# A relational graph layer on one core: products of a tile's end two triples earlier, an edgeless triple left out, a clearing moved, and a small read put ahead of the weights

## The reference

```python
x, src, dst, edge_type = ...      # x [6250, 256]; 200000 edges, sorted by dst; 8 edge types
def gnn(x, edge_index, edge_type, W_rel, W_root, bias):    # three layers
    for l in range(3):
        xr = einsum('nd,rde->rne', x, W_rel[l])
        msg = xr[edge_type, src]
        agg = segment_sum(msg, dst, num_segments=6250)
        x = relu(agg + x @ W_root[l] + bias[l])
    return x
def ffn(x, weight, bias):         # a product through logarithms
    log_x, log_w = log(|x| + 1e-8), log(|weight| + 1e-8)
    acc = exp(log_x - mx) @ exp(log_w - mw).T              # mx, mw: row maxima
    sign = sign(sign(x) @ sign(weight).T)
    return sign * exp(log(acc) + mx + mw.T) + bias
x = x + gnn(layernorm(x), (src, dst), edge_type, ...)
out = x + ffn(layernorm(x), ffn_weight, ffn_bias)
```

## Time and profile before

| | us |
|---|---|
| median of three runs | 6018.02 |
| the three runs | 6017.11 to 6022.20 |
| the profiled execution | 6019.02 |
| its span, first to last instruction | 6017.1 |
| busy: GpSimd | 4448.2 (74%) |
| busy: TensorE, products / weight loads | 4364.5 (73%) / 3933.9 (65%) |
| busy: VectorE | 1827.8 (30%) |
| busy: ScalarE | 619.2 (10%) |
| HBM traffic over the span | 112 GB/s |

### The profile page before, as it was taken

How to read it: one execution, slowest core, us unless ns; L and a number is a source line. 1 busy time by engine, 2 the same in 40 slices (tenths; PEclk the granted TensorE clock), 3 DMA queues, 4 the chain that set the end, 5 groups by cost and what they waited for, 6 DMA issues and landing times.

```text
span 6017.1 us, 84648 instructions
## 1 busy us (share of the span) xinstructions
PE 4364.5 (73%) x26040; PEld 3933.9 (65%) x26041; DVE 1827.8 (30%) x3533; ACT 619.2 (10%) x848; POOL 4448.2 (74%) x4715
## 2 busy tenths in 40 slices
PE   4777777777787777777777767767777777677776
PEld 3666666666676666666666666656666666666666
DVE  4222222222222222222222222223334334333333
ACT  3010010101010000010001000001011011101111
POOL 5777777777777677777777777767777777777775
PEclk9898988898989889898989898988888888888888
DMA  6333333333333333333333333333333333333332
GB/s 194 113 111 113 112 113 111 113 112 113 112 113 112 105 109 108 108 110 107 109 108 109 108 108 109 108 107 110 110 111 112 111 111 113 111 110 113 110 111 84
DMA packets 284200, 672.46 MB, mean 112 GB/s; under 512 B 79916, under 2 KB 133905, under 8 KB 284082
## 3 DMA queue, kind: packets, MB, share of 16 engines
q0 software_dynamic: 225072, 614.90, 35.7%
q1 hardware_dynamic: 30308, 30.00, 1.6%
q10 hardware_dynamic: 28702, 26.46, 1.3%
HBM read 645.36 MB, written 25.68 MB: 112 GB/s over the span
## 4 chain that ended last, share of the span: by engine, by line
POOL 42%; PE 26%; issue 18%; DMA 9%; ACT 2%; DVE 2%; DVEq 2%; ACTq 0%; SPq 0%; POOLq 0%
POOL rows L373 42%; PE bank L391 14%; PE bank L450 10%; DMA rows<-node_table,idx 8%; ACT agg L666 2%; DVE agg L945 1%; PE bank L569 1%; DVE onehot L865 0%; PE bank L495 0%; DVEq L928 0%; DVEq L931 0%; PE bank L567 0%; DVEq L1035 0%; ACT x_in L622 0%; DVEq L945 0%
## 5 line engine op out<-in xcount | busy, mean ns | idle before, releaser
L373 POOL DMA_INDIRECT rows<-node_table,idx x4689 | 4440.9, 947 | 1519.4 <-issue 1316.0
L391 PE MATMUL bank<-onehot,rows 128*128 128x128 f32 x18792 | 2764.7, 308 | 1472.3 <-DMA rows<-node_table,idx 712.8
L391 PEld LDWEIGHTS bank<-onehot,rows 128*128 128x128 f32 x18792 | 2598.6, 220 | 1648.1 <-issue 1629.9
L945 DVE TENSOR_TENSOR agg<-bank,agg 128x256 f32 x1566 | 664.1, 424 | 2172.6 <-PE bank L391 1656.4
L450 PE MATMUL bank<-wrel,agg 128*128 128x256 f32 x5568 | 1273.9, 388 | 14.8 <-issue 8.7
L450 PEld LDWEIGHTS bank<-wrel,agg 128*128 128x128 f32 x5568 | 1079.0, 197 | 164.1 <-issue 17.4
L865 DVE TENSOR_TENSOR onehot<-bank,key 128x1152 f32<-128x1152 f32 x525 | 707.2, 1347 | 0.0
L666 ACT COPY agg<-zero_col 128x2304 f32 x174 | 367.2, 2111 | 3082.4 <-PE bank L450 3082.4
L967 DVE SCALAR_TENSOR_TENSOR acc<-bank,in_first,acc 128x256 f32 x174 | 84.2, 484 | 1897.2 <-PE bank L450 1768.8
L569 PE MATMUL bank<-wroot,nextT 128*128 128x256 f32 x392 | 147.4, 512 | 0.0
L673 ACT COPY acc<-bank 128x256 f32 (+1 forms) x98 | 36.5, 372 | 1052.6 <-PE bank L569 1052.6
(11 more groups left out here) (137 smaller groups left out, 751.6 us busy)
## 6 DMA issues: line engine op xcount, KB each, us to landing
rows<-node_table,idx POOLq DMA_INDIRECT x4689, 2.7
node_table<-new_x ACTq DMA_DIRECT2D x98, 128.0 KB
x_tile<-node_table SPq DMA_DIRECT2D x58, 128.0 KB, 2.2
x_in<-in_x_dram SPq DMA_DIRECT2D x8, 768.0 KB, 11.2
wrel<-in_L_gnn_W_rel_dram SPq DMA_DIRECT2D x6, 1024.0 KB, 7.5
xres<-in_x_dram ACTq DMA_DIRECT2D x48, 128.0 KB
out_dram<-res ACTq DMA_DIRECT2D x48, 128.0 KB
node_table<-x_in SPq DMA_DIRECT2D x7, 768.0 KB, 8.1
```

What stands on the lines that cost most here:

```text
L373: pool.indirect_dma_start(rows[:, s:s + D], None, tables[layer % 2], bass.IndirectOffsetOnAxis(ap=idx[:, g * TPG + k, j:j + 1], axis=0),). ...
L391: last = nc.tensor.matmul(to[:, h, :], of[:, s:s + P], hot[:, hot_k * CH + j, :], start=(j == 0), stop=(j == CH - 1))
L945: nc.vector.tensor_tensor(window, seg[k % 3].rearrange("p h (r w) -> p h r w", r=R), window, ALU.add).then_inc(agg_added, 1)
```

## The change

Five edits, with the bookkeeping of the semaphores for them:

- SyncE reads the triples' span back (58 x 9 values, twice) directly behind its store, ahead of the first layer's weights and the root weights.
- VectorE clears all of agg behind the first one-hots, and not ahead of the feed-forward weights' preparation.
- TensorE has the transposes of a tile's end behind triple 3 (BATCH) and its products behind triple 5 (BATCH + 2), and not behind 4 and 7; layer 0's own two go with them.
- Triple 8 of the last group is not multiplied and not added: TensorE and VectorE only count their semaphores on. In layers 0 and 1 VectorE folds the last group's window ahead of making the next one-hots.
- ScalarE's clearing moves from the end of its part of a group to its start, and clears the half whose transform has just run. It stands so behind new_x and not in front of it.

```diff
@@ SyncE
             sp.dma_start(span_dram.rearrange("m (b p) -> (m b) p", p=P), span_rows[:, :]).then_inc(span_stored, 16)
+            sp.wait_ge(span_stored, 16)
+            for m in range(2):
+                sp.dma_start(span9[:, m, :], span_dram[m, 0:TRIPLES].rearrange("(g k) -> g k", k=TPG)).then_inc(span_loaded, 16)
 
             sp.wait_ge(turned, 11)
             load_weights(0)
...
-            sp.wait_ge(span_stored, 16)
-            for m in range(2):
-                sp.dma_start(span9[:, m, :], span_dram[m, 0:TRIPLES].rearrange("(g k) -> g k", k=TPG)).then_inc(span_loaded, 16)
...
-                sp.wait_ge(out_ready, (layer + 1) * GROUPS)
+                sp.wait_ge(out_ready, (layer + 1) * GROUPS + 1)
@@ TensorE
+            pe.sem_inc(out_ready, 1)
...
+                    if k == TPG - 1:
+
+                        with pe.If(g < GROUPS - 1):
+                            pe.wait_ge(gathered[k], g * (16 * CH) + (layer * (GROUPS - 1) * (16 * CH) + 16 * CH))
+                            pe.wait_ge(agg_added, n + 1)
+                            pe.sem_inc(pe_mark, 1)
+                            products(seg[k % 3], rows, onehot[:, k // BATCH, :, :], k, k % BATCH).then_inc(seg_ready, 1)
+                        with pe.Else():
+                            pe.wait_ge(agg_added, n + 3)
+                            pe.sem_inc(seg_ready, 1)
+                        pe.sem_inc(pe_mark, 1)
+                        continue
...
-                    if late and k == TPG // 2:
+                    if late and k == BATCH:
                         with pe.If(g < late[0]):
                             turn_ended(layer, late[1])
-                    if late and k == TPG - 2:
+                    if late and k == BATCH + 2:
                         with pe.If(g < late[0]):
                             multiply_ended(layer, late[1])
-                    if layer == 0 and k == TPG // 2:
+                    if layer == 0 and k == BATCH:
                         turn(gg)
-                    if layer == 0 and k == TPG - 2:
+                    if layer == 0 and k == BATCH + 2:
@@ ScalarE
                 gg = g + layer * GROUPS
+
+                act.wait_ge(out_ready, gg + 1)
+                act.sem_inc(act_mark, 1)
+                nc.scalar.copy(agg[:, ds((g + 1) % 2 * KH, KH), :, :].rearrange("p h r s -> p (h r s)"),
+                               zero_col[:, :].to_broadcast([P, KH * R * SLOTS])).then_inc(agg_zeroed, 1)
...
-                act.wait_ge(out_ready, gg + 1)
-                act.sem_inc(act_mark, 1)
-                nc.scalar.copy(agg[:, ds(g % 2 * KH, KH), :, :].rearrange("p h r s -> p (h r s)"),
-                               zero_col[:, :].to_broadcast([P, KH * R * SLOTS])).then_inc(agg_zeroed, 1)
@@ VectorE
-            nc.vector.memset(agg[:, :, :, :], 0.0).then_inc(agg_zeroed, 2)
             dve.wait_ge(ffn_loaded, 16)
...
                 make_onehots(0, b).then_inc(onehot_ready, 1)
 
+            nc.vector.memset(agg[:, :, :, :], 0.0).then_inc(agg_zeroed, 1)
...
+                last_group = layer < L - 1 and g == GROUPS - 1
...
+                    def no_edge():
+
+                        dve.wait_ge(agg_added, n + 3)
+                        dve.sem_inc(agg_added, 1)
+
+                    if k < TPG - 1:
+                        add()
+                    elif layer < L - 1:
+                        (add if g < GROUPS - 1 else no_edge)()
+                    else:
+                        with dve.If(g < GROUPS - 1):
+                            add()
+                        with dve.Else():
+                            no_edge()
+                        dve.sem_inc(dve_mark, 1)
+                    if k % BATCH == BATCH - 1 and not (k == TPG - 1 and last_group):
                         make_onehots(g + 1, k // BATCH).then_inc(onehot_ready, 1)
...
                 nc.vector.tensor_tensor(agg[:, half, :, 0:WIN], agg[:, half, :, 0:WIN], agg[:, half, :, P:SLOTS], ALU.add).then_inc(agg_ready, 1)
+                if last_group:
+                    make_onehots(g + 1, BATCHES - 1).then_inc(onehot_ready, 1)
...
-                dve.wait_ge(out_ready, gg + 1)
+                dve.wait_ge(out_ready, gg + 2)
```

## The result

| | before | after |
|---|---|---|
| median, us | 6020.35 (22 runs, 6012.06 to 6024.10) | 6012.24 (22 runs, 6004.08 to 6016.27) |
| ratio | | 0.9985, 95% interval 0.9978 to 0.9991 |
| profiled execution / span, us | 6019.02 / 6017.1 | 6014.94 / 6013.0 |

The change gains 9 us (0.15%, and by the interval between 5 and 13 us). The gain is real, but 22 us were forecast, and the time lies outside the predicted range of 5989 to 6008. Three executions of other rounds took 6312, 7301 and 16894 us; the medians and ratios of this document leave them out.

What follows compares the result with a forecast made beforehand. GpSimd's gather stream (4689 steps of 1.25 us) was taken to bound the kernel, 97% of the span. 6019.0 - 6.8 (head) - 15.9 (ends) + 1.0 (tail) = 5997.3, less 1.0 for the median: 5996 us, range 5989 to 6008.

Steps and rivals of the forecast that it cites:

- The head, 6.8: Before the steady gather stream: earlier span read and later agg clearing shorten GpSimd's 7.49 us ring stall by 6.8, bounds 3 to 7.19.
- The two ends, 15.9: Ends of layers 0 and 1: transforms start 7.2 and 6.7 us earlier, clearing's move gives 2.0; bounds 12 to 17.5.
- ScalarE's clearing: Behind the transform at each layer end: new_x no longer waits for agg's clearing, 1.0 us gained each time.
- the 4.6 us of moved products: End of layer 0: products taken from in front of the transform, 2.3 us hidden in TensorE's idling, 2.3 pushing k=6.
- Inside the layers, gathers: Gathers lengthened by VectorE's all-SBUF instructions: net change 0, bounds 6.9 us less to 16.6 more.
- Rival 3: Last layer's 49 tile ends: shifted operations lengthen gathers; three hits each give 6025 us. Chance 0.03, at half price 0.05.
- Inside the layers, the place of the transposes: Last layer's tile ends: TensorE idles some 2.5 us more waiting for mag, but the ring covers it, cost 0.
- the prediction's signs of being wrong: GpSimd waits over 0.4 us elsewhere, last layer's gathers summing over 1495 us, or table waits over 20 us.
- The tail, +1.0: After the last gather: mag at 5977.0 and the following work equal, 1.0 us added for TensorE's clock; bounds -0.5 to 2.6.
- Rival 4, the ring empties: Last layer: beyond 8.4 us of lag each us costs 48 us; 1 us over gives 6044. Chance 0.02.

Runs made afterwards that it cites:

- the run with the head alone: Kernel before with only the triples' span read ahead of the weights and agg cleared behind the first one-hots: 6020.61 us, ratio 0.9987.

## Why the prediction was wrong

- **The head, 6.8.** Right. 6.4 in one profile, 5.1 in the other; 4.1 (where it was alone) to 7.2 in the others that have the edit. The reload and TensorE's start, on which it hung, came within 0.6 us of their forecast in the first profile and within 1.6 in the second.
- **The two ends, 15.9.** Nearly right: 14.7 and 11.7. The terms for the products and for ScalarE's clearing were right (0.9 of 1.0); missed were 1.0 us of the sequencer's way, and the clock: the sum took 7.14 us for both transforms, but in the twelve profiles layer 0's took it four times and layer 1's eight times, and otherwise 8.1 to 10.0 us. Part of the near hit is luck: the 4.6 us of moved products were read from a profile in which they ran at half clock, and the run with the head alone has ends 4.7 us shorter with nothing changed there. Measured against those, the change's ends gained 10.0 and 7.0 us.
- **Inside the layers, gathers.** The 0 stood: the gathers of the last layer over 0.97 us number 66 before and 68 after, and 34 to 83 in the others. In both, every one of them was issued while VectorE ran an instruction with all its tensors in SBUF. Rival 3 fell.
- **Inside the layers, the place of the transposes.** *This step failed*: "Cost: 0, covered by the ring". It cost 7.1 us in one profile and 10.8 in the other, all in the tail. The size of the idling was right: 212.3 us over 49 tile ends are 4.3 us each, where "2.01 ... and some 2.5 us more" was written:

```profile
L570 PE MATMUL bank<-ident_bf,sgn 128*128 128x128 bf16 x98 | 18.2, 289 | 212.3 <-DVE mag L1040 212.3
```

  But I asked only whether the ring would cover a delay, and not whether the delay is made up before the next one. The loop had a tenth of a microsecond to spare where TensorE ran below full clock, and 1.7 where it didn't; after, it was 35.2 us, so 1.4 us a group remained, were carried on, and were paid at the end of the layer. The lower clock behind the longer wait, which the prediction counted in the tail, was left out here. And none of the prediction's signs of being wrong looked at the tail or at the lag: none of them showed.
- **The tail, +1.0.** The same failure: "equal" compared the last group's order alone, from mag on, and took mag at 5977.0 "in either kernel". From the transposes to the transform's end it was equal indeed, 22.3 us in both profiles against 22.5, and the +1.0 for the clock did not come. But mag was ready later behind the last gather, and the whole was 7.1 and 10.8.
- **Rival 4, the ring empties**, named the right mechanism with the wrong price and the wrong point. The price below the point is not zero but the lag of the last group. And the point is not 8.4 us: I read it from an addition, but a place is freed by the products, which for k=0 end some 14 us before its addition (they begin at 5510.86 in the loop above, and it at 5526.34). By the products the ring had 16.2 us of slack before. The change used up nearly all of it: 4.8 us were left in the first profile and 1.1 in the second, at a triple 4, which stands right behind the transposes. There its products began at 5770.72 and its addition at 5773.82, and the gather that refills its place stands at 5774.58:

```profile
5770.72 4.41 PE L392 MATMUL bank<-onehot,rows 128*128 128x128 f32 x24
...
5773.82 0.42 DVE L962 TENSOR_TENSOR agg<-bank,agg 128x256 f32 x1 [2.60 <-PE bank L392]
...
5774.58 0.95 POOL L373 DMA_INDIRECT rows<-node_table,idx  x1 [0.30 <-issue]
```

  So the ring did cover the delay, but by a microsecond, and not by the "8.4 us" less 2.5. Beyond the point the price is what the kernel with the transposes behind triple 2 showed, 112 us.

With +7.1 to +10.8 for +1.0, the sum would have been 6002 to 6006; the rest to 6012 lies in the ends (1.2 and 4.2 us less than forecast, by the transform's clock and the microsecond) and the head (0.4 and 1.7 less), and in the level of the runs: the kernel before was 2.3 us slower over its 22 runs than in the three shown.

## What to carry to other kernels

A buffer between two streams hides a delay once; a delay in every round is hidden only if the round of the consumer stays shorter than the producer's. So add up the consumer's closed loop (here 32.1 to 33.7 us against 33.8) before an instruction with a wait is moved ahead in it, with the granted clock that TensorE has behind such a wait, and look at how the lag goes over the whole layer, not at whether anybody waits: here no wait of GpSimd showed anything. When an instruction waits for another engine, place it where its input is ready, and count what stands behind it.

## What the runs showed of the hardware

- The indirect gather's own duration differs between profiled executions, 0.946 to 0.949 us in the median (4438 to 4459 us in sum); the changed kernel alone, profiled twice, had 4450.2 and 4441.4 us. That is as much as the change gains.
- A gather gets longer when it is issued during a VectorE instruction that has all its tensors in SBUF: of the 24 issued during an addition of the result (line 1016) before the change, 22 took over 0.97 us, up to 1.195, and of the 658 issued during an addition of a triple, with one input in PSUM, none did.
- The microsecond between the last wait of a TensorE branch and the first matmul behind the loop's end was unexpected (1.03 to 1.08 us); half of it went with an earlier wait.
- Whether TensorE's transform behind 2.2 us of idling runs at full clock (7.14 us) or partly at the lower one (8.5 to 10.0) changes from execution to execution: 7.14 and 8.99 at the end of layer 1 in the two profiles of the changed kernel.
